# Decoder block on one core: the context stage's products in another order, and the first batch's loads and rows at other places of it

## The reference

```
x = x + attn(layernorm(x))            # causal, 16 query heads, 4 key/value heads, low rank, rope
x = x + xattn(layernorm(x), ctx)      # inside: Qn, Kn, Vn = layernorm(...)
      q, k, v = Qn wq, Kn wk, Vn wv   # 16 heads of 64
      out = (l2norm(q) l2norm(k)^T) v # no softmax
      y = Q + out wo + bo ;  y + gelu(layernorm(y) w1 + b1) w2 + b2
x = x + ffn(layernorm(x))             # gelu, ternary weights
```

## Time and profile before

| | |
|---|---|
| median of 3 runs | 1224.75 us (1219.87 to 1226.69) |
| the profiled execution, its own time | 1223.7 us |
| its span, first to last instruction | 1221.9 us |
| PE busy | 1027.8 us, 84% of the span |
| DVE, ACT, POOL busy | 796.7, 650.7, 369.4 us |
| mean granted TensorE clock | 0.927 of full speed |

### The profile page before, as it was taken

The page is one execution under the profiler, slowest core; times in us unless marked ns, Lnnn a source line. Parts: engine busy times, 40 slices in busy tenths (PEclk is TensorE's granted clock), DMA queues, the critical chain, the costliest instruction groups (busy, mean ns, idle before and its releaser), DMA issues. The chain is left out here.

```text
span 1221.9 us, 23498 instructions
## 1 busy us (share of the span) xinstructions
PE 1027.8 (84%) x7133; PEld 766.0 (63%) x7133; DVE 796.7 (65%) x1737; ACT 650.7 (53%) x1155; POOL 369.4 (30%) x516
## 2 busy tenths in 40 slices
PE   3777489999999947866479999999999999998997
PEld 2444334444444416755367878878788787887986
DVE  5888877778787716745265756757566665657554
ACT  1333246777777744543236474464744647455554
POOL 0333368884433320101212132311323112221120
PEclk9777779999999976977779999999999999999999
DMA  3333535553332131446311212101121011010000
GB/s 98 95 117 100 173 118 150 144 145 99 96 93 84 37 105 55 205 182 235 134 51 71 52 69 71 69 17 52 69 69 69 19 50 69 17 69 1 19 1 35
DMA packets 56596, 103.93 MB, mean 85 GB/s; under 512 B 10256, under 2 KB 36368, under 8 KB 52432
## 3 DMA queue, kind: packets, MB, share of 16 engines
q1 hardware_dynamic: 53728, 96.29, 24.2%
q0 software_dynamic: 1920, 6.03, 1.7%
q10 hardware_dynamic: 880, 0.74, 0.2%
HBM read 63.05 MB, written 39.58 MB: 84 GB/s over the span
## 5 line engine op out<-in xcount | busy, mean ns | idle before, releaser
L820 ACT ACTIVATE p_probs<-p_psS 128x512 f32<-128x512 f32 (+1 forms) x352 | 179.6, 557 | 71.0 <-ACTq L819 70.2
L719 DVE CUSTOM_DVE_ANT_0 p_psA<-p_psA,p_mask 128x512 f32<-128x512 f32 (+1 forms) x256 | 155.2, 648 | 61.2 <-DVEq L717 59.8
L1891 DVE TENSOR_TENSOR p_hl<-p_h,p_hh 128x512 fp32r<-128x512 f32 x128 | 100.8, 790 | 120.7 <-DVEq L1890 120.0
L1713 ACT ACTIVATE p_h<-p_psG,w_columns 128x512 f32<-128x512 f32 x128 | 88.2, 689 | 128.6 <-ACTq L1712 127.8
L851 PE MATMUL p_psA<-p_ks,p_qs 96*128 96x512 bf16 (+3 forms) x512 | 141.5, 312 | 13.6 <-PEq L849 12.3
L870 PE MATMUL p_psS<-p_qs,p_ks 99*128 99x256 bf16 (+3 forms) x512 | 129.0, 304 | 18.4 <-PEq L895 12.9
L2174 PE MATMUL p_psY<-p_n,p_hh 128*128 128x256 f32 x512 | 106.4, 291 | 8.3 <-PEq L2165 4.8
L738 POOL TENSOR_SCALAR_AFFINE_SELECT p_probs<-p_probs 128x512 f32<-128x512 f32 x128 | 80.4, 634 | 95.0 <-POOLq L737 94.9
L2174 PEld LDWEIGHTS p_psY<-p_n,p_hh 128*128 128x128 f32 x512 | 85.9, 195 | 16.4 <-issue 15.2
L870 PEld LDWEIGHTS p_psS<-p_qs,p_ks 99*128 99x128 bf16 x512 | 44.2, 98 | 74.3 <-issue 55.4
L881 PE MATMUL p_psO<-p_probs,p_v 128*32 128x512 f32 (+3 forms) x1024 | 84.0, 446 | 4.3 <-PEq L877 4.3
(11 more groups left out here) (260 smaller groups left out, 2759.8 us busy)
## 6 DMA issues: line engine op xcount, KB each, us to landing
p_n<-n_parts SPq DMA_DIRECT2D x16, 1024.0 KB, 6.4
p_qs<-q_parts SPq DMA_DIRECT2D x192, 64.0 KB, 2.2
o_sums<-p_o SPq DMA_DIRECT2D x32, 256.0 KB, 2.1
n_parts<-p_nh SPq DMA_DIRECT2D x8, 1024.0 KB, 3.9
n_parts<-p_nl SPq DMA_DIRECT2D x8, 1024.0 KB, 6.3
q_parts<-p_part SPq DMA_DIRECT2D x48, 128.0 KB
p_x<-in_x_dram SPq DMA_DIRECT2D x8, 512.0 KB, 4.5
p_o<-o_sums SPq DMA_DIRECT2D x16, 256.0 KB
```

The source lines that it names most:

```text
L719: nc.vector.tensor_tensor_reduce(out=bank[:, 0:w], in0=bank[:, 0:w], in1=mask[:, S - w:S], scale=1.0, scalar=MASKED, op0=ALU.add, op1=ALU.max,
L820: nc.scalar.activation(probs[:, g % 2, at:at + n * w], psS[place(s, turn) % SB][:, 0:n * w], ACT.Exp, scale=SCALE).then_inc(exp_done, 1)
L1713: nc.scalar.activation(h[:, s, :], psG[s][:, :], ACT.Gelu, bias=bias[:, m:m + 1])
L1891: nc.vector.tensor_tensor(hl[:, s, :], h[:, s, :], hh[:, s, :].bitcast(F32), ALU.subtract).then_inc(h_parts, 1)
```

## The change

Four tables and lists change; no operation is added or taken away.

- **The list of units.** `M(t, 1, 0)` moves between `N(t, 0, 1)` and `K(t+1, 1)`; `M(t, 1, 1)` follows `N(t, 0, 3)`; both value halves of the next tile stand together ahead of the four quarters of the second factor.
- **SP.** `load_o(0)` is cut in two: sums behind tile 0's stores and the store of the inverses, inverses behind the first store of tile 1. `next_o(1)` moves from behind `load_n(0)` to ahead of the last factor's store.
- **DVE.** The divides move two and one units later, `o_low` one earlier; the constants are set behind `N(2, 1, 3)`; the rows of batch 0 are added behind `N(3, 0, 1)` as before, but ahead of `M(3, 1, 0)`, which now follows there; `z1` moves from behind `N(3, 1, 0)` to behind `N(3, 0, 3)`.
- **PE and ACT.** The attention rows of batch 0 move from behind `M(3, 0, 1)` to behind `N(2, 1, 3)`; the two transposes from behind `N(3, 1, 1)` and `N(3, 1, 3)` to behind `M(3, 1, 1)` and `N(3, 1, 1)`; ACT's two scalings to behind `N(3, 1, 0)` and `N(3, 1, 2)`.

```diff
         for t in range(NTILE):
             follows = t + 1 < NTILE
             units += [(M_, t, 0, 0), (M_, t, 0, 1)]
             units += [(S_, 1)] if t == 0 else []
             units += [(K_, t + 1, 0)] if follows else []
-            units += [(N_, t, 0, 0), (N_, t, 0, 1)]
+            units += [(N_, t, 0, 0), (N_, t, 0, 1), (M_, t, 1, 0)]
             units += [(K_, t + 1, 1)] if follows else []
             units += [(N_, t, 0, 2), (N_, t, 0, 3)]
             units += [(T_, 1, q) for q in range(4)] if t == 0 else []
-            units += [(M_, t, 1, 0), (M_, t, 1, 1)]
-            units += [(V_, t + 1, 0)] if follows else []
-            units += [(N_, t, 1, 0), (N_, t, 1, 1)]
-            units += [(V_, t + 1, 1)] if follows else []
-            units += [(N_, t, 1, 2), (N_, t, 1, 3)]
+            units += [(M_, t, 1, 1)]
+            units += [(V_, t + 1, 0), (V_, t + 1, 1)] if follows else []
+            units += [(N_, t, 1, i) for i in range(4)]
...
             for t in range(NTILE):
                 for z in range(BT):
+                    if (t, z) == (NTILE - 3, BT - 1):
+                        sp.wait_ge(rden_out, 16)
+                        sp.sem_inc(rden_out, -16)
+                        behind["inverses"]()
                     if (t, z) == (NTILE - 2, BT - 1):
                         sp.wait_ge(context_free, 1)
                         sp.sem_inc(context_free, -1)
                         behind["context"]()
+                    if (t, z) == (NTILE - 1, BT - 1):
+                        behind["last"]()
                     sp.wait_ge(n_ready, 1)
...
                     sp.dma_start(scr["rden"].rearrange("b h t -> (b h) t"), sums[:, :]).then_inc(rden_out, 16)
-                if t == NTILE - 3:
-                    sp.wait_ge(rden_out, 16)
-                    sp.sem_inc(rden_out, -16)
+
                     behind["sums"]()
...
-                    if u == (M_, NTILE - 1, 0, 1):
+                    if u == (N_, NTILE - 2, 1, 3):
...
-        DIVIDE_AT, O_HIGH_AT, O_LOW_AT = (("N", 2, 0, 0), ("N", 2, 0, 2)), ("N", 2, 1, 0), ("N", 2, 1, 2)
-        ATTENTION_AT, ROWS_AT, Z_AT = ("M", 3, 0, 1), ("N", 3, 0, 1), ("N", 3, 1, 0)
-        TRANSPOSES_AT = ("N", 3, 1, 1), ("N", 3, 1, 3)
-        FEATURES_AT = ((("N", 3, 1, 2), 0), (("N", 3, 1, 3), 1))
+        DIVIDE_AT, O_HIGH_AT, O_LOW_AT = (("N", 2, 0, 2), ("N", 2, 0, 3)), ("N", 2, 1, 0), ("N", 2, 1, 1)
+        ATTENTION_AT, CONSTANTS_AT, ROWS_AT, Z_AT = ("N", 2, 1, 3), ("N", 2, 1, 3), ("N", 3, 0, 1), ("N", 3, 0, 3)
+        TRANSPOSES_AT, LOW_AT = (("M", 3, 1, 1), ("N", 3, 1, 1)), ("N", 3, 1, 1)
+        FEATURES_AT = ((("N", 3, 1, 0), 0), (("N", 3, 1, 2), 1))
...
-            front({"sums": lambda: load_o(0), "context": constants})
+            front({"sums": lambda: load_sums(0), "inverses": lambda: load_inverses(0), "context": constants,
+                   "last": lambda: next_o(1)})
             load_n(0)
-            next_o(1)
             next_o(2)
```

More of the change, by code:

```diff
@@ L1559, in sync, with load_sums @@
         def sync(sp, front):
-            def load_o(b):
+            def load_sums(b):
                 for c in range(C):
@@ L1563, in load_o, with load_inverses @@
                     sp.dma_start(o[:, c, :], scr["o"][b].rearrange("g (r x) t -> (g r) x t", r=G)[heads, 0:D, :]).then_inc(o_in, 16)
+            def load_inverses(b):
+                for c in range(C):
+                    heads = slice(c * H // C, (c + 1) * H // C)
                     sp.dma_start(ol[:, c, :].bitcast(F32), scr["rden"][b, heads, :].unsqueeze(1).broadcast_to([H // C, D, S])
                                  ).then_inc(o_in, 16)
+            def load_o(b):
+                load_sums(b)
+                load_inverses(b)
             def load_x(b):
@@ L2131, in last_round, with first_constants @@
                 output_rows(TERNARY_7, xin)
-            def first_rows():
+            def first_constants():
                 nc.vector.memset(eps[:, :], EPS)
@@ L2138, in first_rows @@
                 dve.sem_inc(out_done, 16)
-                attention_added(True)
             front({DIVIDE_AT[0]: lambda: divide(0), DIVIDE_AT[1]: lambda: divide(1), O_HIGH_AT: o_high, O_LOW_AT: o_low,
-                   ROWS_AT: first_rows, Z_AT: z1})
-            for c in range(C):
-                affine_low(fl, fh, c)
+                   CONSTANTS_AT: first_constants, ROWS_AT: lambda: attention_added(True), Z_AT: z1,
+                   LOW_AT: lambda: affine_low(fl, fh, 0)})
+            affine_low(fl, fh, 1)
             dve.wait_ge(const_in, 16 * 3)
```

## The result

The changed kernel takes 1205.49 us (median of 4 runs, 1202.89 to 1207.43) against 1222.31 us for the kernel before (4 runs on the same chip): ratio 0.985, interval 0.9821 to 0.9879. The forecast was 1202 us, its own range 1197 to 1207. The program was run in two more sets, called "again" and "third": 1200.21 and 1202.43 us, ratios 0.9823 and 0.9815. The profiled execution took 1206.89 us, 16.8 us less than the one of before.

The account below looks back on a forecast made before the run. PE was taken to be bound by two waits, 9.63 and 15.88 us, for late-loaded sums that DVE divides. From 1223.7 us, -3.5 - 15.9 - 2.85 = -22.2 gave 1201.5; median forecast 1202, range 1197 to 1207 (8 in 10: 1195 to 1210).

Parts of the forecast that it names:

- Batch 1's wait: PE's idle 15.88 us ahead of batch 1's attention rows goes whole, and the half clock behind it, 2.85 us.
- The first divide: DVE's 8.57 us wait at batch 0's first divide goes, since its loads are issued earlier; 4 us of cover.
- The new order: Order of units in tiles 0 and 1: 1.1 us won, 1.7 lost per tile; taken as +0.2 us, bounds -2 and +2.
- Tile 2: From M(2,0,0) to batch 0's attention rows 19.0 us; PE waits 3.1 us there in place of 9.63.
- The attention rows at half clock: Batch 0's attention rows, after PE's 3.1 us wait, take 5.25 us at half clock instead of 2.9: 2.3 us.
- Tile 3 to the first query: Chain over DVE, POOL and ACT, its last part 12.2 us; first query at 573.8, 3.5 us earlier than before.
- The marks of being wrong: Wrong if batch 1's divide starts after 580, the first query is not earlier than 577, or tile 1 exceeds 20.5 us.
- The cast beside POOL's power: DVE's cast of batch 0's sums beside POOL's power over 16 columns takes 0.68 us; bounds 0 and +1.9 us.
- Late loads: Rival: batch 1's loads land 8 us or so later, PE idles 3 us, half clock behind: 1208; chance 0.12.
- First gain eaten: Rival: tile 3's new chain takes 16 us, queries start where they did, only the second wait goes: 1206; chance 0.10.
- Clock kept: Rival: PE keeps full clock at attention rows, first query tiles and last quarters, its waits being short: 1196; chance 0.09.
- The slower one: Rival: short waits ahead of M and N halve the clock in every tile, +30 against -22: 1233; chance 0.04.

Follow-up runs that it names:

- the single moved call: Kernel before with only batch 1's five loads moved ahead of the last factor's store: 1206.97 us, ratio 0.9862.
- the old list: Changed kernel with the list of units as before; loads, divides, rows, transposes and scalings at their new places: 1200.24 us, ratio 0.9834.
- the order alone: Kernel before with the new list of units and nothing else: 1222.31 us (12 runs), ratio 0.9983.
- filled wait: Changed kernel with the last quarter N(t,1,3) of tiles 0 to 2 issued three times over, keeping PE busy ahead of M: 1204.68 us, ratio 0.9844.

## Why the prediction was right, step by step

- **Batch 1's wait** (-15.9, and -2.85 for the clock behind it): right, and shown by the single moved call (17.34 us behind). The two terms together were 1.1 us too small: 17.08 us measured against 18.2. From the first query to batch 1's attention rows are 12.70 us (579.75 to 592.45), where 13.95 were taken from before; the half clock ended after six products (582.45), so the queries gave time back too. In the five profiles in which DVE waits for these loads at their new place, they took 14.2 to 14.6 us from their issue to the divide. The forecast's 15.15 is counted from the factor's load; from the issue of the first sums at 585.02 it was 14.2 us before the change too. So the place in the queue brought the gain, not a shorter transfer. The divide itself waited for no load: DVE came from the queries' rows.
- **The first divide**: right, no wait; the inverses went out at 521.58 and had landed by 540.57. In "again" they went out at 517.87, 4 us later than forecast, and the divide came at 533.80, 3 us later than the 531 forecast, so there was still cover.
- **The new order, +0.2 us within ±2**: right for the total (0.9983, and the same total with the old list). The waits of 0.93 and 0.19 us became 0 and 1.6, forecast 0 and 1.7. But the working doesn't give its own +0.2: 1.1 us won and 1.7 lost are 0.6 us per tile and 1.2 for two. Measured from M(0,0,0) to M(2,0,0) are +2.1, +1.0 and +0.6. The working also left out the clock behind the 1.6 us, and the wait of 1.88 us ahead of `N(1,0,0)` that swallows part of it: tile 1 grew by 1.6 us in the first profile (20.68, over the mark of 20.5) and by 0.2 in the other two.
- **Tile 2, 19.0 us to the attention rows**: 1.15 us too little in two profiles and 4.2 in the first. The place of the wait and its size were right (3.05 us, forecast 3.1). Of the 1.15 us, 1.0 lies ahead of the first divide, which came 10.5 us behind M(2,0,0) instead of 9.5. Half clock behind the wait ahead of M is what came on top in the first.
- **The attention rows at half clock, +2.3**: in "again" and "third" the half clock came, but not for all 24 products: 4.4 and 4.3 us to the next product, forecast 5.25. In the first profile they took 3.0, the other bound. Both are of one program.
- **Tile 3 to the first query**: the chain was right, 2.4 us shorter than forecast in two profiles. Of these 1.5 lie between the end of `z` and the first query (10.67 instead of 12.2). What the forecast didn't price is PE's idle time in this chain, the 7.43 us ahead of the transpose: with the quarters put there, 3 to 5 us come back. The forecast said that no other idle time of PE was as long as the two it named; that is so, but the 5.01 us at 564.75 stood in this chain before, and it didn't ask what becomes of them.
- **The marks of being wrong.** All three were passed in the first profile: batch 1's divide at 580.81 (mark 580), the first query at 579.75 (577), tile 1 at 20.68 us (20.5). In "again" none was (575.47, 574.41 and 19.36), nor in "third". Without the start of M(0,0,0), 3.6 us later than before, the first two would have been kept; the third is the clock of tile 1. Marks given as absolute times and read from one profile can't tell scatter from a wrong mechanism.
- **The cast beside POOL's power** at 0.68 us: right. The power shows on POOL's timeline:

```profile
543.85 3.17 POOL L1135 TENSOR_TENSOR p_rn<-p_n,p_mhalf 128x16 f32<-128x16 f32 x1 [18.75 <-POOLq L1134]
```

It ran to 547.02, and the cast at 546.04 took 0.68 us, the divide at 543.58 0.69 us; the power took 3.17 instead of 2.90 us. The Trainium skill (GPSIMD Engine Reference, Specifications) tells of contention without regard to size; by that rule 1.9 us would have been lost here, and they were not. Beside the addition of 1024 columns it holds: 2.67 us for the cast at 582.48. In the kernel with the old list the pair of divides fell beside that addition too (POOL from 572.27), and took 3.47 instead of 1.53 us:

```profile
572.09 3.47 DVE L1853 TENSOR_TENSOR p_o<-p_o,p_ol 128x512 f32<-128x512 f32 x2
```

**The sum**: -22.2 us forecast from M(0,0,0) to the last head sums. Measured are -21.0 (98.31 and 17.08 against 99.43 and 36.98), -23.8 and -24.3. In the first profile the scattered start took 3.6 of it. The sum is nearer than its terms: the queries came out 1.1 us and tile 3 2.4 us shorter than forecast, tile 2 1.15 and the first two tiles 0.4 to 0.8 us longer in "again" and "third", and that these cancel is luck. The medians gained 16.8, 21.1 and 22.1 us in the three sets against 22.75 forecast; in the first set the kernel before came out 2.4 us lower than the 1224.75 that the forecast started from, and that brought 1205.49 nearer to 1202 than the gain alone would have.

**The rivals.** Late loads: no, not in the changed kernel. First gain eaten: in two profiles no (95.52 and 95.02 us in front against 99.43), though the first alone (98.31) looks like it. Clock kept: in part, in tile 2 in two profiles and at the attention rows in one. The slower one had its mechanism right in part and its size wrong: waits of 1.6 us were followed by half clock, but for 3 to 7 us, not for the whole tile. It put 9 us on each tile, and tile 1 grew by 1.6 and 0.2; the clock of tile 1 read 0.83 to 0.91, not under 0.7.

**What stays open.** Which of several short waits is followed by half clock. The first profile and the second have the same waits and differ in it. The length alone does not decide: the wait of 1.6 to 1.7 us ahead of tile 1's M was followed by half clock in all four profiles that have it (three of the change, one of the order alone), and the longer one of 1.88 us ahead of `N(1,0,0)` in the profile of before was not, nor the 1.91 us above. The forecast read that stretch as if it held only waits of 0.93 and 0.19 us. That filling the wait ahead of M takes the half clock away was seen in one profile; the kernels with waits of 1.37 and 1.52 us there had none in tile 2's first part either. Why M(0,0,0) starts up to 9 us apart was not tried.

## What to carry to other kernels

Look in the issuing queue for the load that the longest wait ends on, and ask whether anything but its place in the program keeps it there: one call moved ahead of a store brought 1.4% of the 1.5 to 1.9%. Test each part of a change alone; here the loads did all the good that can be shown and the order of products none, and the moved transposes left a gap in which PE had nothing to do until the last quarters were put there. Compare pieces from a common start, in more than one profile, when a gain is of the size of the scatter.

## What the runs showed of the hardware

- Half clock behind a short wait varies between executions of one program: behind 1.61 to 1.69 us idle it was at half for 6 to 7 us, 3 to 4 us or not at all, and behind 3.05 us the next 24 products took 3.0 us or 4.4.
- The longer wait is not the one with half clock behind it: 1.88 and 1.91 us ahead of `N(1,0,0)` were followed by full clock (kernel before and filled wait), 1.61 us ahead of tile 1's M by half clock in "again", "third" and the order alone.
- DVE's operations slow down 2 to 4 times beside POOL's addition of 1024 columns (divide pair 3.47 for 1.53, cast 2.67 for 0.68), and not beside a power over 16 columns, which itself takes 3.17 for 2.90.
- Batch 1's sums and inverses take 14.2 to 14.6 us from issue to the divide that waits for them in five profiles at the new place, and 13.6 to 14.2 in three profiles at the old one.
